# Last stage of a two-layer gated block: tokens sorted by expert in two phases, against four masked experts

## What is computed

```python
# layer 1, feed-forward; h = layernorm(x), H = 256, I = 1024, E = 4
expert = argmax(h @ W_router)              # one expert per token, lowest index on ties
inner  = gelu(h @ W1[expert] + b1[expert]) # 256 -> 1024, by the token's expert
y      = inner @ Wo + bo                   # 1024 -> 256, one matrix for all
x      = x + tanh(g) * layer_norm(y + h, gamma, beta)
```

## Time and profile before

| what | value |
|---|---|
| median of 3 runs | 936.2 us (930.4 to 936.54) |
| the profiled execution's own time | 929.45 us |
| its span in the profile | 927.6 us |
| mean granted TensorE clock | 0.946 of full |
| TensorE busy | 830.7 us |
| VectorE, ScalarE, GpSimd busy | 578.5, 438.6, 249.8 us |

### The profile page before, as it was taken

How to read it: one execution, slowest core, us unless ns; L and a number is a source line. 1 busy time by engine, 2 the same in 40 slices (tenths; PEclk the granted TensorE clock), 3 DMA queues, 4 the chain that set the end, 5 groups by cost and what they waited for, 6 DMA issues and landing times. The chain is left out here.

```text
span 927.6 us, 11844 instructions
## 1 busy us (share of the span) xinstructions
PE 830.7 (90%) x4356; PEld 493.6 (53%) x4356; DVE 578.5 (62%) x932; ACT 438.6 (47%) x821; POOL 249.8 (27%) x277
## 2 busy tenths in 40 slices
PE   6885999999989889975999999964999999999984
PEld 3442344343337678752443334323778778778764
DVE  4573899999516936576898999738815136036026
ACT  2222788888855376502788878873210210210110
POOL 2130555455532286501000000115211120120220
PEclk9996999999999999987899999995999999998998
DMA  7695222222032300263145322020000000000000
GB/s 269 173 218 163 64 74 74 71 70 71 2 104 81 89 1 0 71 160 91 52 119 169 120 72 71 3 63 1 2 0 1 1 23 1 1 23 1 0 24 23
DMA packets 40539, 60.67 MB, mean 65 GB/s; under 512 B 7257, under 2 KB 17241, under 8 KB 40481
## 3 DMA queue, kind: packets, MB, share of 16 engines
q1 hardware_dynamic: 37216, 55.84, 21.2%
q0 software_dynamic: 864, 0.92, 1.3%
q10 hardware_dynamic: 2400, 3.15, 1.0%
HBM read 40.02 MB, written 18.87 MB: 63 GB/s over the span
## 5 line engine op out<-in xcount | busy, mean ns | idle before, releaser
L1118 DVE TENSOR_REDUCE row_max<-ps_wide 128x2 f32<-128x1024 f32 x256 | 301.2, 1220 | 31.5 <-PE ps_wide L479 25.1
L829 ACT ACTIVATE probs<-ps_a 128x512 f32<-128x512 f32 x342 | 191.5, 602 | 42.4 <-PE ps_a L535 37.3
L479 PE MATMUL ps_wide<-stack_k,stack_q 48*128 48x512 f32 x512 | 154.3, 470 | 15.8 <-DVE row_max L1118 11.3
L535 PE MATMUL ps_a<-stack_q,stack_k 62*128 62x512 f32 (+1 forms) x342 | 139.4, 456 | 11.8 <-ACT probs L829 11.4
L549 PE MATMUL ps_out<-probs,vals 128*17 128x512 f32 x1024 | 135.6, 604 | 0.5 <-POOL probs L978 0.5
L932 ACT ACTIVATE hid_full<-ps_a 128x512 f32<-128x512 f32 x32 | 19.1, 598 | 216.1 <-PE ps_a L748 154.5
L535 PEld LDWEIGHTS ps_a<-stack_q,stack_k 62*128 62x128 f32 (+1 forms) x342 | 60.8, 190 | 99.5 <-ACT probs L829 71.9
L829 ACT ACTIVATE probs<-ps_misc 128x512 f32<-128x512 f32 x170 | 102.4, 603 | 18.0 <-PE ps_misc L535 13.8
L978 POOL TENSOR_TENSOR probs<-probs,fixes_sb 128x512 f32<-128x512 f32 x64 | 81.9, 1280 | 82.7 <-ACT probs L829 82.7
L1037 POOL TENSOR_TENSOR hid_lo<-hid_full,hid_hi 128x512 fp32r<-128x512 f32 x32 | 42.5, 1331 | 192.8 <-ACT hid_hi L933 192.8
L479 PEld LDWEIGHTS ps_wide<-stack_k,stack_q 48*128 48x128 f32 x512 | 62.3, 190 | 52.5 <-DVE row_max L1118 21.0
(11 more groups left out here) (166 smaller groups left out, 1236.2 us busy)
## 6 DMA issues: line engine op xcount, KB each, us to landing
planes_k<-planes SPq DMA_DIRECT2D x32, 256.0 KB, 3.8
planes_q<-planes SPq DMA_DIRECT2D x32, 256.0 KB, 3.8
stack_q<-planes_q SPq DMA_DIRECT2D x64, 128.0 KB, 2.8
stack_k<-planes_k SPq DMA_DIRECT2D x64, 128.0 KB, 2.8
stack_q<-planes_q SPq DMA_DIRECT2D x64, 64.0 KB, 2.7
stack_k<-planes_k SPq DMA_DIRECT2D x64, 64.0 KB, 2.6
w_e_raw<-in_L_W SPq DMA_DIRECT2D x4, 1024.0 KB, 5.4
w_raw<-in_L_W SPq DMA_DIRECT2D x2, 1024.0 KB, 6.2
```

The costliest lines, as they stand in the source:

```text
L479: mm(raw_slot(("pair", g, p))[:, i * S:(i + 1) * S], stack_q[at, slot(g, c) + q * P:slot(g, c) + (q + 1) * P], stack_k[at, slot(g, c):slot ...
L535: mm(score_slot(("tile", n))[:], stack_k[at, slot(g, c) + k * P:slot(g, c) + (k + 1) * P], stack_q[at, slot(g, c):slot(g, c) + S], start=T ...
L829: do(probs[n % PROBS][:, j, :], score_slot(("tile", n * HG + j))[:], ACT.Exp, scale=0.25).then_inc(exp_done, 1)
L1118: v.tensor_reduce(row_max[:, g % 2, :, p], raw_slot(("pair", g, p))[:].rearrange("p (i k) -> p i k", i=2), AX, ALU.max).then_inc(sem(f"max ...
```

## The change

The last stage no longer masks. Tokens are placed by expert into regions of a table of token numbers in device memory, each expert's region is cut into blocks of 128, and 19 blocks (16, and 3 for regions that are not full) are worked one after the other, each with one expert's weights. Empty places hold a number outside the tokens, which the transfers skip.

- Routing of rows 0 and 1 stands inside attention's last two groups on TensorE, ScalarE and VectorE, that of rows 2 and 3 ahead of and in the block loop. count sums one-hots over tokens with products, so that each token gets its place; place and tables on VectorE make places, the experts of the blocks and the rows of the table. Phase 0 has the first 5 blocks and uses tokens 0 to 1023 alone; phase 1 has the other 14.
- GpSimd writes token numbers by indirect transfers (place_ids, 16 of 128 elements), reads them back in block order (fetch_ids), gathers each block's normed and plain tokens (2 KB a token) from a copy in device memory that SP stores (keep_rows), and scatters each finished block to the output. A gather into a slot of the ring of 8 waits until that slot's scatter has landed.
- Up: tokens are now the stationary side and 512 inner features the moving side, 12 products and 2 of bias per block, whose weight address comes from a register loaded per block (value_load). Gelu gives tokens by features; eight transposes turn it back, in two groups of four that stand between the halves of the previous block's down products. Down: 24 products of 256 columns per block.
- GpSimd splits the expert weights (in 16 pieces, copy and subtraction), the output weights and the expert bias during attention 1; SP's loads for the stage are issued in group 6 (load_last). The ring of attention weights has four entries in layer 1 instead of six. One more table (the blank places) is written ahead of attention 0.

```diff
+REGION = B * S // P
+BLOCKS = REGION + E - 1
+EARLY_ROWS = 2
+FIRST = QT * EARLY_ROWS - E + 1
+SECOND = BLOCKS - FIRST
+ROWS = REGION * E + E
+NOBODY = 2 * B * S
+ROW_RING = 8
+WEIGHTS_FROM = 6
+LANDING = 4
...
+PROBS = (6, 4)
...
+def count(b):
+    bank = count_bank(b)
+    slot_free("count", b)
+    pe.wait_ge(sem("routed"), b + 1)
+    wait(pe, sem("counts_kept"), b)
+    before = table[:, START:PART] if b == 0 else running[:, b - 1].rearrange("p t e -> p (t e)")
+    mm(bank[:, 0:QT * E], sums[:, 1, :], before, start=True, stop=False)
+    for t in range(QT - 1):
+        mm(bank[:, (t + 1) * E:QT * E].rearrange("p (t e) -> p t e", e=E), sums[:, 1, :],
+           onehot[:, b * QT + t, :].unsqueeze(1).broadcast_to([P, QT - 1 - t, E]), start=False, stop=False)
+    mm(bank[:, 0:QT * E], sums[:, 0, :], onehot[:, b * QT:(b + 1) * QT, :].rearrange("p t e -> p (t e)"),
+       start=False, stop=True).then_inc(sem("counted"), 1)
...
+if l == 1 and (g, k) == (G - 1, 0):
+    count(1)
+    total(0)
...
+if l == 1 and (g, k) == (G - 2, 1):
+    turn_n3(0)
+if l == 1 and (g, k) == (G - 2, 2):
+    turn_n3(1)
+    route_logits(0)
+if l == 1 and (g, k) == (G - 2, 3):
+    route_logits(1)
+    count(0)
...
+wait(pe, sem("hid1_ready"), 2 * n)
+pe.wait_ge(sem("offset_ready"), 1 + int(n >= FIRST))
+at = nc.tensor.value_load(offset[0:1, n:n + 1], min_val=0, max_val=(E - 1) * C * FF)
+for half in range(2):
+    bank = pw[0][:, half * S:(half + 1) * S]
     for i, (r, w) in enumerate(PRODUCTS):
-        if u == 0 and w == 1:
-            pe.wait_ge(sem("w1_low"), len(LOWS_POOL))
-            pe.wait_ge(sem("w1_low_dve"), len(LOWS_DVE))
-        for e in range(E):
-            if f == 0 and w == 0:
-                pe.wait_ge(sem("masked_done"), (2 * b + r) * E + e + 1)
-            for c in range(C):
-                mm(ps[u % 2][:], w1_parts[w][:, e, c, f * P:(f + 1) * P], masked[r][:, e, c, :],
-                          start=(i == 0 and e == 0 and c == 0), stop=False)
-    if u == 0:
-        pe.wait_ge(sem("b1_split"), 1)
-    mm(ps[u % 2][:], b1_parts[0:HOT, f * P:(f + 1) * P], onehotT[0:HOT, b % 2, :], start=False, stop=True
+        if half == 0 and i == 0:
+            pe.wait_ge(sem("sorted_high"), n + 1)
+        if half == 0 and i == 2:
+            pe.wait_ge(sem("sorted_low"), n + 1)
+        for c in range(C):
...
+        mm(bank, sortedT[r][:, n % 2, c, :], w1_flat[w][:, bass.ds(at + (c * FF + half * S), S)],
+           start=(i == 0 and c == 0), stop=False)
+mm(bank, select[0:HOT, n, :], b1_parts[0:HOT, half * S:(half + 1) * S], start=False, stop=True
...
+turn_n3(2)
+route_logits(2)
+turn_ids(0)
+count(2)
+turn_rows(0)
+pe.wait_ge(sem("w1_low"), E * 4 + 2)
+pe.wait_ge(sem("b1_split"), 1)
+pe.wait_ge(sem("selected"), 1)
+for n in range(BLOCKS):
+    if n == FIRST:
+        pe.wait_ge(sem("selected"), 2)
+    up(n)
+    if n + 1 < BLOCKS and n != FIRST - 1:
+        turn_rows(n + 1)
+    if n == 0:
+        turn_n3(3)
+    if n == 1:
+        route_logits(3)
+    for half in range(2):
+        if n > 0:
+            down(n - 1, range(half * FC // 2, (half + 1) * FC // 2))
+        turn_hidden(n, (half,))
+    if n == 1:
+        count(3)
+        total(1)
+    if n == FIRST - 2:
+        turn_ids(1)
+    if n == FIRST - 1:
+        turn_rows(n + 1)
+down(BLOCKS - 1)
...
+if l == 1 and j == 2 and g == G - 2 and k - 2 in range(EARLY_ROWS):
+    if k == 2:
+        act.wait_ge(sem("b1_split"), 1)
+    rows1(k - 2)
...
+rows_high(0)
+for n in range(BLOCKS):
+    for half in range(2):
+        act.wait_ge(sem("up1_done"), 2 * n + half + 1)
+        wait(act, sem("hid1_turned"), 2 * n - 3 + half)
+        do(hid1[:, n % 2, half * S:(half + 1) * S], pw[0][:, half * S:(half + 1) * S], ACT.Gelu
+           ).then_inc(sem("hid1_ready"), 1)
+    if n + 1 < BLOCKS and n != FIRST - 1:
+        rows_high(n + 1)
...
+def halves(hi, lo, raw, n):
+    v.tensor_copy(hi, raw).then_inc(sem("w1_high"), 1)
+    pool.wait_ge(sem("w1_high"), n + 1)
+    v.tensor_tensor(lo, raw, hi.bitcast(F32), ALU.subtract).then_inc(sem("w1_low"), 1)
...
+if l == 1 and g == WEIGHTS_FROM + E:
+    roots(3, 0)
+if l == 1 and g == G - 3:
+    hidden_weights()
...
+if l == 1 and g >= WEIGHTS_FROM:
+    for n in range(3 * (g - WEIGHTS_FROM), min(3 * (g - WEIGHTS_FROM) + 3, E * QT)):
+        expert_weights(*divmod(n, QT))
+if l == 1 and g == WEIGHTS_FROM:
+    split_bias()
...
+def place_ids(b):
+    pool.wait_ge(sem("dest_ready"), b + 1)
+    for t in range(b * QT, (b + 1) * QT):
+        nc.gpsimd.indirect_dma_start(ids_dram.rearrange("r (p o) -> (r p) o", o=1), bass.IndirectOffsetOnAxis(dest[:, t:t + 1], 0),
+                                     table[:, TOKENS + t:TOKENS + t + 1], None).then_inc(sem("ids_sent"), 16)
...
+    wait(pool, sem(f"gathered_{n % LANDING}"), 16 * (n // LANDING))
+    if n >= ROW_RING:
+        pool.wait_ge(sem(f"stored_{n % LANDING}"), 16 * ((n - ROW_RING) // LANDING + 1))
+    nc.gpsimd.indirect_dma_start(sorted_rows[n % ROW_RING][:], None, rows_dram[0:known, :], bass.IndirectOffsetOnAxis(ids[:, n:n + 1], 0),
+                                 bounds_check=known - 1, oob_is_err=False).then_inc(sem(f"gathered_{n % LANDING}"), 16)
+def scatter(n):
+    pool.wait_ge(sem("x_final"), n + 1)
+    wait(pool, sem(f"stored_{n % LANDING}"), 16 * (n // LANDING))
+    nc.gpsimd.indirect_dma_start(out, bass.IndirectOffsetOnAxis(ids[:, n:n + 1], 0), sorted_rows[n % ROW_RING][:, D:2 * D], None,
+                                 bounds_check=B * S - 1, oob_is_err=False).then_inc(sem(f"stored_{n % LANDING}"), 16)
+roots(3, 1)
+place_ids(0)
+roots(3, 2)
+place_ids(1)
+fetch_ids(0)
+for n in range(FIRST):
+    gather(n)
+roots(3, 3)
+place_ids(2)
+place_ids(3)
+fetch_ids(1)
+for n in range(2):
+    root4(n)
+for n in range(3):
+    gather(FIRST + n)
+for n in range(2, BLOCKS + 2):
+    if n < BLOCKS:
+        root4(n)
+    scatter(n - 2)
+    m = n + ROW_RING - 2
+    if FIRST + 3 <= m < BLOCKS:
+        gather(m)
...
+normal(3, 0, x)
+normalise(G - 4)
+normal(3, 1, x)
+route(0)
+place(0)
+route(1)
+place(1)
+for t in tiles(2, None):
+    update3(t)
+aggregate(3, 2, 1e-5)
+normalise(G - 3)
+tables(0)
+normal(3, 2, x)
+normalise(G - 2)
+normalise(G - 1)
...
+def hidden_low(n):
+    for half in range(2):
+        dve.wait_ge(sem("hid1_high"), 2 * n + half + 1)
+        fs = slice(half * FC // 2, (half + 1) * FC // 2)
+        v.tensor_tensor(hid1T[1][:, n % 2, fs], ps[half][:].rearrange("p (f t) -> p f t", t=P), hid1T[0][:, n % 2, fs].bitcast(F32),
+                        ALU.subtract).then_inc(sem("hid1_low"), 1)
+def residual(n):
+    dve.wait_ge(sem("down1_done"), n + 1)
+    back = sorted_rows[n % ROW_RING][:, 0:D]
+    v.tensor_tensor(back, po[:, 0:D], back, ALU.add).then_inc(sem("down1_read"), 1)
...
+for n in range(BLOCKS + 2):
+    if n == FIRST - 1:
+        keep_ids(1)
+    if n + 1 < BLOCKS and n != FIRST - 1:
+        rows_low(n + 1)
+    if 0 < n <= BLOCKS:
+        residual(n - 1)
+    if n < BLOCKS:
+        hidden_low(n)
+    if n == 1:
+        route(3)
+    if n == 2:
+        place(3)
+        tables(1)
+    if n == 3:
+        finish(0)
+    if n > 2:
+        finish(n - 2)
+    if 0 < n <= BLOCKS:
+        spread(n - 1)
```

More of the change, by code:

```diff
@@ L13 @@
 F16 = mybir.dt.float16
+U32 = mybir.dt.uint32
+I32 = mybir.dt.int32
 P = 128
@@ L496, in attention, with total @@
+            def total(phase):
+                b = (EARLY_ROWS, B)[phase] - 1
+                pe.wait_ge(sem("counts_kept"), b + 1)
+                mm(totals_bank(phase)[:, 0:E], sums[:, 1, :], running[:, b, 0, :], start=True, stop=True).then_inc(sem("totals_done"), 1)
             def attention(l):
@@ new lines, in turn_hidden, with down @@
+            def turn_hidden(n, halves=(0, 1)):
+                for half in halves:
+                    pe.wait_ge(sem("hid1_ready"), 2 * n + half + 1)
+                    wait(pe, sem("hid1_low"), 2 * n - 1 + half)
+                    for f in range(FC // 2):
+                        at_f = (half * FC // 2 + f) * P
+                        last = tr(ps[half][:, f * P:(f + 1) * P], hid1[:, n % 2, at_f:at_f + P], ident[:])
+                    last.then_inc(sem("hid1_turned"), 1)
+            def down(n, fs=range(FC)):
+                if fs[0] == 0:
+                    wait(pe, sem("down1_read"), n)
+                for f in fs:
+                    if f % (FC // 2) == 0:
+                        pe.wait_ge(sem("hid1_low"), 2 * n + f // (FC // 2) + 1)
+                    for i, (r, w) in enumerate(PRODUCTS):
+                        last = mm(po[:, 0:D], hid1T[r][:, n % 2, f, :], w_mo_part(w, f),
+                                  start=(f == 0 and i == 0), stop=(f == FC - 1 and i == 2))
+                if fs[-1] == FC - 1:
+                    last.then_inc(sem("down1_done"), 1)
@@ L1375, in _, with keep_ids @@
-            for q in range(QT + 1):
-                if q < QT:
-                    residual((B - 1) * QT + q)
```

(9 more changed lines are left out.)

632 lines of the change are left out of this document (369 added, 263 removed).

## The result

The changed kernel takes 873.3 us (median of four, 870.8 to 875.1) where the kernel before takes 935.4 (median of four, 930.4 to 936.5): ratio 0.934, 95% interval 0.930 to 0.939, some 62 us. Forecast were 842 us, range 815 to 880. The sign and the range held; the time came out 31 us above the forecast, and the profile shows errors in the working of both signs: some 50 us of delay that it had not counted, and 19 us for a register read that cost nothing.

The account below looks back on a forecast made before the run. TensorE, busy 90% of the span, was taken as the bound before and after; 645 + 150.9 + 4.5 + 3 + 6 + 19 + 1 + 11 = 840.4 us of span, plus 1.85 outside it, gave 842 us, range 815 to 880.

Parts of the forecast that it names:

- the register read: Block loop: TensorE sits out 1.0 us per block reading its expert's offset, 19 us in all (0 to 32).
- the blank table: Ahead of attention 0: one more transfer, issue 0.5 and at most 3 more landing, taken as 1 us.
- The bound and TensorE per block: Block loop: TensorE sets the pace with 7.94 us of work per block, 150.9 us for 19 blocks.
- rival A: Block loop: VectorE, waiting for GpSimd, becomes the bound at 10.5 us a block, 872 us; chance 0.21 (860 to 885).
- Rival B: Block loop: the register costs nothing, 823 us; chance 0.17 together with a faster start (under 828).
- Without them TensorE would wait some 0.6 twice a block, 23 us: Block loop: splitting the down products around the hidden transposes hides Gelu and the copy, saving TensorE 23 us.
- The landing of the token numbers, 2.8 us, "covered by 4 us": Start: GpSimd's eight scatters and a fetch run from 614, ready at 634, 4 us before they are needed.
- At the switch the term was 6: Switch to the second phase: gather about 1 late, last count 1, late token numbers; 6 us (0 to 15).
- Attention's end, "+7": Attention's last two groups: added routing on TensorE and ScalarE, partly hidden, costs 7 us; attention ends at 628.
- Group six, "hidden" and "0": Attention's group six: GpSimd's bias work and SP's loads delay nothing, 0 us, because maxima are wanted later.
- The end, 9 us from the last down product: Tail: residual 0.46, spread 1.29, root 0.75, finish 2.64, scatter 0.7 and 2.8, together 9 us.
- Half clock at the first products, 3: Block loop's start: the first products run at half clock, costing 3 us (0 to 7).

Follow-up runs that it names:

- e3: Changed kernel with up-product weight addresses fixed when the program is built, no register read: 866.7 us, ratio 0.931 to the kernel before.
- e1: Changed kernel with all eight hidden transposes together behind the previous block's down products: 867.8 us, ratio 0.933 to the kernel before.
- e2: Changed kernel with all eight hidden transposes together ahead of the previous block's down products: 870.5 us, ratio 0.935 to the kernel before.
- e9: Changed kernel plus six batches of scatters alone behind its end, rows of 4, 64 and 512 bytes, each waited for; its time as a whole says nothing.
- e12: e11 plus token numbers written as 64-byte rows, turned earlier, and block 5's rows at their usual place: 830.9 us, ratio 0.891 to the kernel before.
- e8: Changed kernel with VectorE's fourth-row routing ahead of a residual, its placement and tables at the start of block 2: 854.1 us, ratio 0.913 to the kernel before.
- e11: Changed kernel with the edits of e5, e6 and e8 together: 847.1 us, ratio 0.908 to the kernel before.
- e4: Changed kernel with the expert bias cleared in group 8, loaded in 9 and split in 11: 868.5 us, ratio 0.934 to the kernel before.
- e5: e4's bias move plus the seven other loads spread over groups 6 to 8, against the changed kernel: 863.5 us, ratio 0.923 to the kernel before.
- e6: Changed kernel with the second row's token-number scatters issued ahead of the third row's root: 870.7 us, ratio 0.933 to the kernel before.
- e7: Changed kernel with the third row's stores held until the first phase's token numbers are fetched: 870.1 us, ratio 0.932 to the kernel before.
- e10: Changed kernel plus sixteen unread 512-column products between the narrow routing pieces at attention's end: 876.0 us, ratio 0.936 to the kernel before.

## Why the prediction was right, and where it was wrong

The span came out at 871.1 us against a sum of 840.4. By stretches: the first up product 20.9 us late (665.9 against 645); from there to block 6 81.7 us where the terms give 67.1 (six periods of 7.94, six reads, 4.5, 3 and 6), +14.6; twelve steady blocks 95.1 against 107.3, -12.2; from the start of the last block's up products to the end 28.3 against 19.9, +8.4; the blank table 0 against 1, -1.0. Together +30.7. (The steps listed for the start add up to 644.1 and not to 645.) Without the 19 us for the register read the sum would have been 50 us short; that 873 lies inside 815 to 880 is in part luck, since the two errors partly cancel.

- **The bound and TensorE per block: right.** 7.94 forecast, 7.93 measured; in e3, e1 and e2 too TensorE is busy throughout the steady loop. VectorE has 2.0 us to spare where 1.7 was forecast. The scaling takes 0.46 us, so rival A (VectorE locked out by GpSimd, 872 us) is refuted, though the measured time fell into its band: the same number by another cause. The Trainium skill's lock rule (SBUF — State Buffer, Who interferes with whom), which made it a rival, costs this loop at most 0.05 us a scaling (0.46 against 0.41).
- **The register read, 1.0 us a block: wrong**, it is 0 in the loop (e3), -19 over 19 blocks. It was taken from a bound by a transfer's landing, and no row showed the read itself. Rival B was right on this; its 823 was missed only for the other errors.
- **"Without them TensorE would wait some 0.6 twice a block, 23 us": wrong.** Gelu was compared with the twelve products beside it, and not with the whole distance between a block's up and down products (e1, e2).
- **The landing of the token numbers, 2.8 us, "covered by 4 us": the largest wrong step.** It took 16.8 and 7.7 us. The row it was taken from moves 128 KB in rows of 2 KB or more; a scatter of 4-byte rows behaves otherwise (e9). At the start, attention's end to the first up product took 22.3 us where the forecast had 17, and 10.1 in e12. At the switch the term was 6, and the three periods from block 3 on took 23.8 us more than at 7.93 each. Asking earlier gives 20 us back (e8), wider rows and the order they allow 16 more (e12 against e11).
- **Attention's end, "+7": half of it.** From the last maximum to the last transposes it took 41.2 us against 24.7 before, +16.5; the other 6.2 us of its delay are group six. The work was counted at the full clock, and the clock was at 0.50 from 615.3 to 635.8. An estimate from this: 20 us at half the clock hold at most 10 us more than at the full one, which would cover the missing 9.5; no run kept the clock up, so it isn't shown.
- **Group six, "hidden" and "0": wrong, 4 to 8 us.** The prediction had the work right (SP holds the maximum until GpSimd has cleared the bias buffer, "some 8 us" into the group; it was 7.6) and the overlap wrong: "wanted at the group's end: 0". The maximum's transfer stands in SP's queue behind the loads and takes 5.3 us to land, so TensorE had it 14.3 us after the split at 516.2, in a group of 11 (e4, e5).
- **The end, 9 us from the last down product: 16.5** (854.6 to 871.1). VectorE's list puts the finish of block 17 between the residual and the spread of block 18 (3.0 us), and the residual behind another spread (1.2): the listed steps were right, what stood between them was left out. The last scatter lands 2.1 us after its issue, at 867.8, and the span runs on for 3.3 us in which the profile shows no instruction.
- **Half clock at the first products, 3: right** (7.2 us instead of 3.7), but there are two more such stretches, from 690 to 697 and on and off from 718 to 745, each behind a pause.

## What to carry to other kernels

Price a transfer by the row with the same run length, not the same size: an indirect write of 4-byte rows took 6.9 us and more where 64-byte rows took 1.2, and it delays other transfers; pad such rows (64 bytes were enough here). An instruction that prepares a later stage is free only if every queue it stands in, SP's too, has room ahead of the next thing that is due. Where work of block n - 1 stands between two steps of block n, their order among themselves is free: look for the pauses at the seams instead, where each costs its length and often a stretch at half clock.

## What the runs showed that was not expected

- Landing after the last issue, on an idle core (e9): with rows of 4 bytes 6.9 us for 1 scatter, 19.3 for 4 and 18.2 for 8; with rows of 64 bytes 1.2 for 4 and for 8. The records of the data's transfers in the profile end some 1 to 2 us after the last issue; what is late is the completion that GpSimd waits for.
- Two 512 KB stores land in 18 us (12 in e6) while such scatters are open and in 3.0 and 4.1 to 4.9 us when they aren't (e12, e7).
- An indirect issue costs GpSimd 0.93 to 1.13 us and 0.3 to the next, where a plain one took 0.70.
- TensorE's granted clock fell from 1.00 to 0.50 although the engine had not stood for longer than 0.45 us, and stayed there while it was busy all the time (e10: 100% from 620 to 625 us, at 0.50); sixteen wide products among the narrow ones didn't keep it up; behind a pause of 2.5 us (687.8) it fell, and without that pause (e8) the same work ran at 1.00.
- A read of an offset into TensorE's register, with twelve products addressed by it, costs nothing in a loop where TensorE is never idle.
